# A decoder layer on one core: the opening rebuilt, self rows projected first, later self tiles done in quarters

## What is computed

```python
# 1. self: attention within one row, between its 16 head dimensions
q = einsum('bse,edh->bsdh', x, Wq) + bq        # 16 x 32; k, v: 16 x 8, repeated 4 times
scores = einsum('bsdh,bseh->bsde', q, k) / sqrt(16)
out = einsum('bsde,bseh->bsdh', softmax(scores), v)
x = layernorm(x + out)
# 2. cross attention: 32 query heads, 8 key/value heads of 128, keys = context and x itself
kv = concatenate([context, x], axis=1)         # 1857 rows
q, k = rms_norm(x @ Wq), rms_norm(kv @ Wk); v = kv @ Wv
x = layernorm(x + softmax(q k^T / sqrt(128)) v @ Wo)
# 3. router of 64 experts, top 8 of a softmax, mixed biases
x = layernorm(x * w_sum + w_dense @ expert_bias)
```

## Time and profile before

| | us |
|---|---|
| median of three runs | 2953.23 |
| the profiled execution's own time | 2952.19 |
| its span in the profile | 2950.4 |
| TensorE busy in the span | 2800.4 (95%) |
| GpSimd busy | 2418.5 (82%) |
| VectorE busy | 2178.1 (74%) |
| ScalarE busy | 2069.0 (70%) |

### The profile page before, as it was taken

The page is one execution under the profiler, slowest core; times in us unless marked ns, Lnnn a source line. Parts: engine busy times, 40 slices in busy tenths (PEclk is TensorE's granted clock), DMA queues, the critical chain, the costliest instruction groups (busy, mean ns, idle before and its releaser), DMA issues. The chain is left out here.

```text
span 2950.4 us, 46837 instructions
## 1 busy us (share of the span) xinstructions
PE 2800.4 (95%) x14860; PEld 2242.9 (76%) x14860; DVE 2178.1 (74%) x3447; ACT 2069.0 (70%) x3867; POOL 2418.5 (82%) x2271
## 2 busy tenths in 40 slices
PE   4669999999999999999999999999999999999976
PEld 2458888888888888888888888888888888888744
DVE  5677777777777777777777778777777777777855
ACT  2137777777777777777777777777777777777741
POOL 4548888888888888888988888888898888888880
PEclk7779999999999999999999999999999999999985
DMA  6224434333434433333434343334334333333101
GB/s 236 90 93 143 144 128 139 127 127 129 147 122 157 133 130 131 132 131 130 143 125 154 129 137 132 129 127 138 127 122 138 113 115 113 109 108 115 65 8 68
DMA packets 154885, 367.69 MB, mean 125 GB/s; under 512 B 12682, under 2 KB 46476, under 8 KB 154641
## 3 DMA queue, kind: packets, MB, share of 16 engines
q1 hardware_dynamic: 152888, 362.87, 37.1%
q10 hardware_dynamic: 1752, 1.84, 0.2%
HBM read 327.95 MB, written 36.70 MB: 124 GB/s over the span
## 5 line engine op out<-in xcount | busy, mean ns | idle before, releaser
L1170 DVE SCALAR_TENSOR_TENSOR running_max<-S_ps,rk,running_max 128x512 f32<-128x512 f32 (+1 forms) x896 | 669.6, 747 | 251.0 <-ACT scores L912 243.2
L912 ACT ACTIVATE scores<-S_ps,rk 128x512 f32<-128x512 f32 (+1 forms) x960 | 653.8, 681 | 225.9 <-PE S_ps L652 220.9
L570 POOL TENSOR_TENSOR P_lo<-late,P_hi 128x512 fp32r<-128x512 f32 x512 | 675.2, 1319 | 129.2 <-ACT late L928 129.2
L1154 DVE TENSOR_TENSOR scores<-scores,Mb_ps 128x512 f32<-128x512 f32 (+1 forms) x960 | 648.8, 677 | 166.4 <-PE Mb_ps L797 166.4
L588 POOL TENSOR_TENSOR late<-late,scores 128x512 f32<-128x512 f32 (+1 forms) x448 | 587.4, 1311 | 119.5 <-ACT scores L928 76.9
L650 PE MATMUL S_ps<-QT_hi,KT_hi 128*128 128x512 f32 (+1 forms) x960 | 560.3, 584 | 15.1 <-DVE running_max L1170 13.9
L588 POOL TENSOR_TENSOR late<-late 128x512 f32<-128x512 f32 x384 | 525.0, 1367 | 0.0
L650 PE MATMUL K_ps<-Wkv_hi,kvT 128*128 128x256 f32 (+1 forms) x1664 | 473.6, 285 | 2.9 <-DVE V_full L1210 2.9
L652 PE MATMUL K_ps<-Wkv_hi,kvT 128*128 128x256 f32 (+1 forms) x1664 | 473.7, 285 | 0.0
L651 PE MATMUL K_ps<-Wkv_lo,kvT 128*128 128x256 f32 (+1 forms) x1664 | 473.1, 284 | 0.0
L680 PE MATMUL OT_ps<-scores,V_full 128*128 128x512 f32 (+1 forms) x896 | 462.1, 598 | 0.0
(11 more groups left out here) (198 smaller groups left out, 5447.7 us busy)
## 6 DMA issues: line engine op xcount, KB each, us to landing
kvT<-kvT_scratch SPq DMA_DIRECT2D x416, 512.0 KB, 3.3
w_stage<-in_L_xattn_Wq SPq DMA_DIRECT2D x64, 512.0 KB, 4.3
w_stage<-in_L_xattn_Wo SPq DMA_DIRECT2D x64, 512.0 KB, 4.3
kvT_scratch<-built SPq DMA_DIRECT2D x58, 512.0 KB, 2.8
xrow<-in_ctx SPq DMA_DIRECT2D x48, 256.0 KB
w_stage<-in_L_xattn_Wk SPq DMA_DIRECT2D x32, 256.0 KB, 2.8
w_stage<-in_L_xattn_Wv SPq DMA_DIRECT2D x32, 256.0 KB, 3.3
xT<-kvT_scratch SPq DMA_DIRECT2D x6, 512.0 KB, 5.7
```

The costliest lines, as they stand in the source:

```text
L570: e.tensor_tensor(P_lo[n % 2][0:r, :], P_sb[n % 2][0:r, :], f(P_hi[n % 2][0:r, :]), ALU.subtract)\
L912: e.activation(row[s % RING][0:r, :], S_ps[s % 2][0:r, :], ACT.Copy, scale=rk[0:r, v % 2, j:j + 1])\
L1154: e.tensor_tensor(d, d, Mb_ps[0:r, :], ALU.add).then_inc(s_d, 1)
L1170: e.scalar_tensor_tensor(a, src, k, a, ALU.mult, ALU.max).then_inc(s_top, 1)
```

## The change

The opening gets its own table of jobs, `OPENING`, from step -16 to 9. The row tiles of the context are built from step -16 on, one a step, and written into `tile`, the buffers from which unit 0 projects: `project` takes them there, from step -13 on, without a load. They are still stored for the other seven units of the batch. Key tiles 12 and 13 of unit 0 are its own rows (`rows_at`), and its queries and scores come where the table has them. Step 10 is unit 1's first, as before.

All 8 self tiles are turned and projected in steps -15 to -7. Tiles 0 and 1 are finished at once, in steps -13 to -9. The q, k and v of tiles 2 to 7 are stored to a scratch in HBM. Each is loaded again later with its rows of `x` and done in 14 events (`EVENTS`: steps whose oldest tile in work is key tile 2, 6 or 10, from step 24 on): four quarters of products on GpSimd, each with its sum on VectorE a step later, the softmax, four quarters of value products, the residual and norm. All eight quarters are GpSimd's.

`P_sb` is gone: the exponential of a `HALF` tile stays in its ring row too, so `copy_scores` waits for `lo` and `add` of the row's old tile instead of its exponential, and `exp` waits no longer for `add`. Six semaphores instead of two watch the stores of row tiles. Tiles are loaded five steps ahead of use throughout. GpSimd's splits come before its self products in a step. Cut to its core:

```diff
+    OPENING = {
+        -16: [("X", 0, 2)],
+        -15: [("X", 0, 3)],
+        -14: [("X", 0, 4)],
+        -13: [("KV", 0, 0), ("X", 0, 5)],
+        -12: [("KV", 0, 1), ("X", 0, 6)],
...
+        -9: [("KV", 0, 4), ("X", 0, 9)],
+        -8: [("KV", 0, 5), ("KT", 0, 0), ("X", 0, 0), ("X", 0, 1)],
+        -7: [("Q", 0, 0, 0), ("Q", 0, 0, 1), ("X", 0, 10)],
+        -6: [("Q", 0, 1, 0), ("Q", 0, 1, 1)],
+        -5: [("KV", 0, 6), ("X", 0, 11)],
...
+        -1: [("KV", 0, 10), ("QT", 0, 0), ("X", 0, 14)],
+        0: [("KV", 0, 11)],
...
+        3: [("KV", 0, 14)],
+        5: [("KT", 0, 3)],
+        6: [("X", 1, 2)],
+        7: [("QT", 0, 1)],
+        9: [("X", 1, 3)],
+    }
     def splits(s):
...
+        if s < CYCLE_0:
+            chunk = {-16: ("Wkv", 0, 0), -15: ("Wq", 0, 0), -8: ("Wq", 0, 1), 1: ("Wkv", 1, 0), 4: ("Wq", 1, 0),
+                     7: ("Wq", 1, 1)}.get(s)
...
+        SELF_AT[[-15, -15, -13, -12, -11, -10, -9, -8][t]].append(("turn", t))
+        SELF_AT[[-14, -13, -12, -11, -10, -9, -8, -7][t]].append(("project", t))
+    for t in range(TPB):
+        for k, part in enumerate(("products", "scores", "normalise", "residual", "layernorm")):
+            SELF_AT[-13 + k].append((part, t))
+    EVENTS = [s for s in range(WAIT + 4, LAST) if (s - WAIT) % NJ in (2, 6, 10)]
+    LATER = collections.defaultdict(list)
+    for t in range(TPB, SELF):
+        at = EVENTS[14 * (t - TPB):14 * (t - TPB) + 14]
+        LATER[at[0] - 3].append(("load", t, 0))
+        for i in range(4):
+            LATER[at[i]].append(("qk", t, i))
+            LATER[at[i] + 1].append(("qk sum", t, i))
+            LATER[at[6 + i]].append(("pv", t, i))
+            LATER[at[6 + i] + 1].append(("pv sum", t, i))
+        LATER[at[4] + 1].append(("max", t, 0))
...
         def prob(t):
-            return row[t % RING] if t % NJ in FULL else P_sb[half_no(t) % 2]
+            return row[t % RING]
...
@@ sync @@
             load_rows(0, TPB)
-            load_rows(0, TPB + 1)
             for chunk in CHUNKS[:2]:
                 weights(chunk)
+            load_rows(0, TPB + 1)
+            load_self(2)
+            load_self(3)
             for s in STEPS:
...
+                    if part == "project" and t >= TPB:
+                        store_qkv(t)
+                for part, t in SELF_AT[s]:
+                    if part == "turn" and TPB <= t < SELF - 2:
+                        load_self(t + 2)
...
-                if s >= -AHEAD and c % 2 and 5 <= (c + 5) // 2 < NJ and v < UNITS:
-                    load_tile(v, (c + 5) // 2)
...
+                for x in fill(s + 5):
+                    if x[0] == "KV" and x[1] and x[2] >= TPB:
+                        load_tile(x[1], x[2])
@@ gpsimd @@
+            def later_products(part, t, i):
+                n = 8 * (t - TPB) + i + (4 if part == "pv" else 0)
+                if n % 8 == 0:
+                    e.wait_ge(sb_ld, 32 * (t - TPB + 1))
+                if n % 8 == 4:
+                    e.wait_ge(sb_pr, t - TPB + 1)
+                if n:
+
+                    e.wait_ge(sb_r, n)
...
@@ tensor, project @@
+                if v == 0:
+                    e.wait_ge(s_fr, F_AT["X", 0, rows_at(0, j)] + 1)
...
+                    n = LOAD_AT[v, j]
+                    if v:
+                        e.wait_ge(s_kd[n % 3], loaded(n))
                     src = tile[n % 3][:]
@@ scalar, copy_scores, exp, high @@
                     if t % NJ in HALF:
-                        e.wait_ge(s_p, t + 1)
+                        e.wait_ge(s_lo, half_no(t) + 1)
                     else:
                         e.wait_ge(s_pv, t + 1)
-                        e.wait_ge(s_acc, acc_no(t + 1 if t % NJ == 0 else t))
+                    e.wait_ge(s_acc, acc_no(t + 1 if t % NJ == 0 else t))
...
-                        old = half_tile(n - 2)
-                        e.wait_ge(s_pv, old + 1)
-                        e.wait_ge(s_acc, acc_no(old + 1 if old % NJ == 0 else old))
+                        e.wait_ge(s_pv, half_tile(n - 2) + 1)
...
+                        if b == 0:
+                            if k >= 3:
+
+                                e.wait_ge(s_kt, LOADS[k - 3][1] + 1)
+                                e.wait_ge(s_xs[(k - 3) % 6], 16 * ((k - 3) // 6 + 1))
+                            dst = tile[k % 3][:, 0, :, 0:r]
```

More of the change, by code:

```diff
@@ L140, in attention @@
     for t in range(SELF):
[L141 to L149, removed]
+        SELF_AT[[-15, -15, -13, -12, -11, -10, -9, -8][t]].append(("turn", t))
[14 more added lines that the diff above has]
+        LATER[at[4] + 1].append(("max", t, 0))
+        LATER[at[4] + 2].append(("exp", t, 0))
+        LATER[at[5] + 1].append(("normalise", t, 0))
+        LATER[at[10] + 1].append(("residual", t, 0))
+        LATER[at[11] + 1].append(("variance", t, 0))
+        LATER[at[11] + 2].append(("rsqrt", t, 0))
+        LATER[at[12] + 1].append(("newton", t, 0))
+        LATER[at[12] + 2].append(("layernorm", t, 0))
+        LATER[at[12] + 5].append(("store", t, 0))
     STEPS = range(FIRST, LAST)
@@ L496, in _ @@
                         store_x1(t)
-                for part, t in SELF_AT[s + 1]:
-                    if part == "turn" and t >= 2:
-                        load_self(t)
-                if s == -AHEAD + 3:
+                    if part == "project" and t >= TPB:
[3 more added lines that the diff above has]
+                        load_self(t + 2)
+                if s == WAIT:
                     load_y(0)
@@ L634, in _ @@
                     newton(kind, v)
+                for chunk in splits(s):
+                    split(chunk)
                 for part, t in SELF_AT[s]:
@@ L639, in _ @@
                         self_values(t)
-                for chunk in splits(s):
-                    split(chunk)
+                for part, t, i in LATER[s]:
+                    if part in ("qk", "pv"):
+                        later_products(part, t, i)
         @block.tensor
@@ L714, in queries @@
                 k = K_AT["Q", v, t]
+                if v == 0 and part == 0:
+                    e.wait_ge(s_fr, F_AT["X", 0, t] + 1)
                 if part == 0:
@@ L1077, in _ @@
                         self_rsqrt(t)
+                for part, t, _ in LATER[s]:
+                    if part == "exp":
+                        later_exp(t)
+                    elif part == "rsqrt":
+                        later_rsqrt(t)
         @block.vector
@@ L1261, in _ @@
             for s in STEPS:
-                if s < -AHEAD:
-                    for part, t in SELF_AT[s]:
-                        if part in SELF_STAGE:
-                            SELF_STAGE[part](t)
+                for part, t in SELF_AT[s]:
+                    if part in SELF_STAGE:
+                        SELF_STAGE[part](t)
                 if 0 <= s - WAIT < NS:
@@ L1282, in _ @@
                         OT_low(x[1])
-                if s >= -AHEAD:
-                    for part, t in SELF_AT[s]:
-                        if part in SELF_STAGE:
-                            SELF_STAGE[part](t)
+                for part, t, i in LATER[s]:
+                    later(part, t, i)
 def feed_forward(nc, y_in, Wr, rb, eb, out):
```

334 lines of the change are left out of this document (219 added, 115 removed), and 7 rows, old and new, of the table OPENING.

## The result

The changed kernel took **2918.28 us** (median of four runs, 2915.38 to 2921.62) against 2952.64 for the kernel before on the same chip: a ratio of 0.9884, 95% interval 0.987 to 0.9897, so 34 us less. The forecast was 90 us less, and the time lies above the range of 2845 to 2898.

What follows compares the result with a forecast made beforehand. The prediction took TensorE to bound the steady steps, with 96.35 us of its idle time in the opening. Opening 100 us earlier, less 10 us of later stalls, gave 90 us less: 2863 us, range 2845 to 2898.

Steps and rivals of the forecast that it cites:

- Part 1: Opening up to the first self projection: it begins at 19 us and is read out at 25.5.
- Part 2: Opening, batch 0's chain of tiles 0 and 1: TensorE's idle and gates up to step 10 together cost 11 us.
- The other gates: Opening, waits besides the long idle: 0.3, 1.4, 0.8, 0.8 and 1.3 us, plus 3 us over steps 4 to 9.
- Part 3: Opening, SyncE's queue and loads: waits for self turns and stores cost nothing (18 us if uncovered); DMA share 0.6, no bound.
- The sum: Opening total: 25.5 + 70.4 + 11 + 3 us for the clock puts step 10 at 110 us, 100 earlier.
- Part 4: Steady steps, six later self tiles in quarters: GpSimd's lateness costs 10 us (bounds 0 and 77), DVE sums nothing.
- The term that was worked out: Steady steps: GpSimd's 48 quarters delay later `lo` operations that TensorE waits for, 10 us in all.
- (a): Rival: opening goes cold or waits for its transfers, step 10 at 125 to 150, 2878 to 2903 us; chance 0.21.
- (b): Rival: half of the opening's gates and no stall later, 109 us less, 2845 to 2850 us; chance 0.12.
- (e): Rival: unit 0 still projects late, its buffers waiting for stores; 46 us gained less 10, 2917 us; chance 0.02.
- (c): Rival: GpSimd becomes the bound or holds DVE by their shared way to SBUF, 2893 to 2941 us; chance 0.05.
- (d): Rival: slower than before, quarters at 2.4 us plus sums at 0.6 cost 144 us, 2997 us; chance 0.02.

Runs made afterwards that it cites:

- no_later: The change with the six later self tiles only loaded and stored, their products, sums, softmax and norm left out (measures only): 2848.13 us.
- sums_without_wait: The change with each later-tile sum reading the loaded rows instead of GpSimd's products, so VectorE never waits for the quarter (measures only): 2860.17 us.
- quarters_only: The change with GpSimd's 48 quarters kept, VectorE's and ScalarE's part of the later tiles left out (measures only): 2855.99 us.
- sums_one_later: The change with each of the 48 VectorE sums two steps after its GpSimd quarter instead of one: 2862.34 us.
- residual_one_later: Batch 0's residual and layernorm stages one step later; base: the change with later quarters at four places per cycle, sums three steps behind: 2848.00 us against 2851.93.

## Why the prediction was wrong, point by point

**The opening was right.** The steps and gates of the change's own trace:

```profile
18.52 2.82 PE L889 MATMUL OT_ps<-scores 128*128 128x384 f32 x8
21.27 0.91 PE L890 MATMUL OT_ps<-scores 1*128 1x384 f32 x2
...
53.90 1.09 PE L869 MATMUL F_ps<-ident,xrow 128*128 128x128 f32 x4 [4.16 <-DVE kvT L1421]
...
108.92 0.50 PE L772 MATMUL S_ps<-QT_hi,KT_hi 128*128 128x512 f32 x1 [0.70 <-DVE running_max L1364]
```

- *Part 1.* The first projection begins at 18.5 (19 forecast) but ends at 22.1, not 25.5: it took 3.6 us. The 6.36 us of before were matmuls at half the speed, 5.46 for eight where the second projection's eight took 2.85, and the sum carried that price over although the other, 3.6, stood beside it. The stretches of the two projections in the kernel before (columns as above) show the granted clock at 1.00 in both, so this column doesn't tell the slow one:

```profile
22.08:28.44 6.36, 6.36 (x10) 2.92 (x10) 0.09 (x1) 0.94 (x2) 0.00 (x0) 1.00 0.37 137
28.44:32.06 3.62, 3.62 (x12) 1.73 (x11) 1.29 (x2) 0.49 (x1) 2.94 (x2) 1.00 0.00 0
```

- *Part 2.* The long idle was forecast at 3.5 us near 52 and is 4.16 at 53.9, released by the drain that was named. The other gates were forecast at 4.6 us and 3 for steps 4 to 9; the trace has 1.11, 0.78, 1.07, 0.69 and 1.19, and 2.3. All together 11.3 against 11.
- *Part 3.* From the first projection on TensorE waits for no self row and no built tile. ScalarE waits 9.6 us for stores up to step 10, and none of it reaches TensorE, as was argued. The DMA share is 0.56, 0.6 was forecast. Right.
- *The sum.* Step 10 at 108.92, forecast 110. That it fits to 1 us is in part luck: the first projection was 3.4 us too long, and what stands beside the gates (22.1 + 70.4 + 11.3 = 103.8 leaves 5.1 us) was put at 3. `no_later` shows that the 101 us are kept to the end.

**Part 4 failed, in one sentence.** It said that the DVE sums "stand behind its maxima, in its 24% of idle time, and cost nothing". Their 0.69 us each (0.57 forecast) do cost next to nothing: 4.2 us with all the rest. But a sum begins with a wait for GpSimd, and this wait had no term. All numbers were there: GpSimd is up to two steps late, said the same part, and a sum comes one step behind its quarter; so VectorE can wait a step or more, with a shift and a maximum behind it. The loss of this wait is 58.1 us (`sums_without_wait`). The prediction named the sign of it too, TensorE waiting for copies of the maximum in the steady steps, and that sign came, 42.2 us of it, but no term of the sum stood for it. What is queued behind a waiting instruction was named for SyncE and ScalarE, not for this wait. VectorE's idle time as a total was no cover: the 230.8 us that it waits for ScalarE's copies are some 400 pieces, none over 1.5 us, and what decides is how soon TensorE needs what is queued behind the wait.

**The term that was worked out was right.** GpSimd's lateness at `lo` was put at 10 us; `quarters_only` less `no_later` is 7.9. With that, 2953 - 101 + 8 + 4 = 2864 would have been the time but for the wait, and `sums_one_later` is 2862.

**The rivals.** (a), a cold opening, did not come: the clock is 0.97 up to step 10. (b), half of the gates and no stall later, did not come: the gates are there in full, and so are the stalls. (e) gave 2917, 1 us from the measured time, and that is chance: it has unit 0 project late, and step 10 comes 101 us earlier, not 46. (c) gave 2893 to 2941, where the time lies, but by another way than the measured one: neither GpSimd's load nor a shared way to SBUF. The means of GpSimd's own `add` (1336 ns in `no_later`, 1332 in `quarters_only`, 200 to 1600 us) and of VectorE's maximum (747 in both) don't move. Two of VectorE's operations with both inputs in SBUF move, one up and one down (see the last section). The whole of the quarters costs 7.9 us, not 88. By the Trainium skill ("SBUF — State Buffer", Who interferes with whom) one of VectorE and GpSimd blocks the other for an operation's length on a port pair that they share; whether part of the 7.9 us is that, no run here separates. (d) decided from 2.08 us lost per quarter; the measured loss over `no_later` is 70.2 / 48 = 1.46, nearer to that than to the forecast's 0.2, but not by its mechanism: it priced how long the quarter and the sum take, and with both in place and no wait the later tiles cost 12 us (2860.17 against 2848.13).

**The idle time was not all.** From step 10 on the change lost 69 us of its lead. TensorE's idle time is 2809.6 less 2708.4 busy = 101 us behind step 10, where it was 2740.2 less 2686.5 = 54: that is 47 of it. Another part is its clock, which stood at half beside ten of its long waits. A stretch at full clock ahead of it, one right behind the 3.07 us of idle time, and the next:

```profile
244.00:247.00 3.00, 2.53 (x16) 2.06 (x15) 0.44 (x2) 2.12 (x4) 2.86 (x3) 1.00 0.35 139
251.00:253.80 2.80, 2.80 (x7) 1.77 (x8) 2.71 (x5) 2.19 (x4) 2.80 (x3) 0.50 0.02 5
254.40:257.40 3.00, 3.00 (x13) 2.14 (x12) 1.34 (x2) 1.20 (x2) 3.00 (x3) 1.00 0.43 130
```

There are ten such stretches of 3.4 us between 120 and 2700 us, each worth 1.7 by estimate: some 17 us. The kernel before had none from 209 to 2700 us. The remaining 5 us are in TensorE's busy time (2708.4 against 2686.5 behind step 10, of which the clock is 17) and I can't place them. The view of one line shows the same without windows: the key/value matmuls (122 to 2700 us; least, median, longest ns) reach 418 in the change; in `sums_one_later` the longest is 287.

```profile
L772 PE MATMUL K_ps<-Wkv_hi,kvT x1572: 274/282/418, 121.8 to 2699.5; 128*128 128x256 f32 x182, 128*65 128x256 f32 x15
```

## What to carry to other kernels

When work is moved to an engine that runs late, price the consumer's wait, not only the operation: the wait is as long as the producer is behind, and everything queued behind it on the consumer's engine is late with it. The consumer's idle time as a total says nothing of it. A wait of 3 to 4.6 us cost TensorE 2.3 to 3.1 us ahead of an operation that TensorE needed next, and waits of up to 3.96 us right behind that operation cost nothing, so ask of each place what the next need is. Here a sum two steps behind its quarter instead of one, with nothing else changed, gave back 56 us of the 58 that the wait cost.

## What the runs showed of the hardware

- TensorE's granted clock went to half beside single idle pieces of about 2 to 4 us in a kernel that otherwise keeps it busy (0.50 from 251.0 to 253.8, behind 3.07 us), but not beside each: of 17 pieces of 1.7 us and more in the change behind 120 us, ten had it, and the 2.59 us that end at 183.9 and the 2.76 that end at 1221.6 had not. In the opening it came behind 4.16 us:

```profile
54.00:57.00 3.00, 3.00 (x8) 2.09 (x9) 2.82 (x10) 0.60 (x1) 0.00 (x0) 0.50 0.69 236
```

- With 2.1 us less of idle time in one place, `residual_one_later` reached step 10 4.8 us earlier. Its granted clock is at half for 3.4 us there (from 59.3), that of its base for 6.8 (from 52.5); by estimate this is 1.7 of the other 2.7, and 1.0 is left open.
- Matmuls took twice their later time at a granted clock of 1.00 early in the kernel before (eight in 5.46 us, the next eight in 2.85).
- 48 products of 128 x 512 on GpSimd left the means of VectorE's operations that read a bank as they were. Of those with both inputs in SBUF, `OT_lo` became faster (mean 1519 ns, then 1338) and `natq` slower (200 to 1600 us; busy, mean ns, idle before; `no_later`, then `quarters_only`); why is not shown:

```profile
L1374 DVE TENSOR_TENSOR natq<-natq,rq 128x512 f32<-128x512 f32 x34 | 44.9, 1358 | 0.0
L1377 DVE TENSOR_TENSOR natq<-natq,rq 128x512 f32<-128x512 f32 x34 | 47.9, 1447 | 0.0
```
